# A recurrent scan with expert work in its gaps: the work one step later, and the first gate inputs taken from SBUF

## The chip, the cores and the metric

One NeuronCore of a Trainium2 chip runs the whole program. The metric is device time in microseconds (us), the median of several executions; lower is better.

## What is computed

The input x has 8 sequences of 512 tokens with 256 channels. First comes a mixture of experts with a residual: one shared gated MLP and, for each token, the best 2 of 8 small experts. Then a gated recurrent unit (GRU) runs over the 512 tokens of each sequence, again with a residual.

```python
shared = silu(xf @ w1) * (xf @ w3) @ w2
combine = top-2 gates of sigmoid(concat(xf, cond) @ router_W), normalised
h = gelu(einsum('nc,ech->enh', xf, W1e)); y = einsum('enh,ehc->enc', h, W2e)
x = x + (shared + einsum('ne,enc->nc', combine, y)) / 3
Xz, Xr, Xh = x @ Wxz.T + bxz, x @ Wxr.T + bxr, x @ Wxh.T + bxh
for t in range(512):                 # H is 8 x 256
    Z = sigmoid(Xz[t] + H @ Whz.T + bhz)
    R = sigmoid(Xr[t] + H @ Whr.T + bhr)
    H = Z * H + (1 - Z) * tanh(Xh[t] + (R * H) @ Whh.T + bhh)
    Y[t] = H @ Whq.T + bhq
x = x + Y
```

## The kernel before

**Tiles and steps.** The tokens are cut in 32 tiles; tile n holds 16 time steps (TS) of all 8 sequences, 128 rows. The scan has 512 steps, named by (n, s): step s, 0 to 15, of tile n. The expert work of a pair of tiles is laid in the gaps of the scan's steps, well ahead of the steps that need it.

**One step of the scan** (the functions `body` of each engine). TensorE (PE) makes the product for R into `r_bank` and that for Z into `zc_bank` (L1235), then runs a first filler (`fill_up`), then the third product from `rhT`, then a second filler (`fill_rest`). ScalarE (ACT) takes the tanh of R (L685) and of Z (L687), copies the gate inputs of the next step into `r_bank` (`seed_r`, L608), makes `a_row` (L696), takes the tanh of the third product (`t_h`, L705) and copies the other gate inputs (`seed_zc`, L616). VectorE (DVE) transposes `t_r` (L974), makes `rhT` (L977), transposes `a_row` into `factors` (L980), makes `terms` (L991), transposes `t_h` (L996) and updates the state with two scans into `hist` (L999). Each engine takes its instructions in this order, so a wait on one instruction holds all behind it.

**The order of the filler is written out by hand.** `place_of(n, s)` (L375) turns a step into a pair p and a slot r from 0 to 31, since a pair of tiles spans 32 steps:

```python
sp = s + TS * ((n + 1) % 2)
return (n + 1) // 2 + (sp >= FIRST_STEP), (sp - FIRST_STEP) % SPAN
```

FIRST_STEP is 6, so slot r lies in step s = (r + 6) mod 16. Tables by slot say what each slot holds: `UP_GAP2` gives 5 matmuls of the up projections (L1100), 6 in the slots of `SIX_UPS`, 3 in two; `DOWNS1` the down projections (L1073); `PROJ1` the gate input projection of a tile in slots 2 to 5 and 18 to 21; `BIAS2` its bias add on DVE after the state update of slots 3, 5, 19 and 21 (L855); `HIDDEN1` a DVE product (L812) between `factors` and `terms`, in slot 8 among others; `TANH1` = 25 a small tanh of the router on ACT ahead of `t_h` (L565). What is tied to s and not to r: `keep_states`, an ACT copy of the 16 states of the tile before, in step s = 0 ahead of `t_h` (L623); the wait for a tile's gate inputs.

**How gate inputs travel.** The projection leaves `xproj` in SBUF with a row for each token. SyncE's queue (SP) stores it in two halves (q = 0, 1) in DRAM (`store_inputs`, L466), waits until a half has landed, and loads it back with 4 DMAs in the layout that a step reads, `xs` (`gate_rows`, L472). It does that for the first 8 time steps of a tile and later for the other 8. `seed_r` of the next tile's first step lies in step s = 15 and waits for the first part:

```python
if last:
    act.wait_ge(xs_first, 16 * NG * (n + 2))
seed_r(*after)
```

So for every tile boundary the bias add in step s = 11 (slots 5 and 21) starts a chain of store, landing, load, landing, which must be done by ACT's `seed_r` in step s = 15.

**The head** runs tile 0's experts and much of tile 1's before step (0, 0): the down projections of slots 6 to 9, and the first 36 matmuls of the next pair's up projections (`FIRST_UPS`). Tile 0's gate inputs go the same way through DRAM, and SP loads the second part when the first has landed. In the tail, when no filler is left, `keep_busy` (L1239, L1243) gives PE two matmuls in a gap; a gap of slot 0 in tile 31 has none.

Of the kernel before, what the change touches and what calls it, by code (L numbers as in the profile page):

```python
# [17 lines left out]
def moe_then_gru(nc, x, cond, router_w, router_b, w1, w3, w2, we1, we2,  # L18
# [7 lines left out]
    B, T, C = x.shape  # L26
    P = 128
    TS = P // B
# [8 lines left out]
    NG = 4  # L37
    GW = C // NG
    Q = 32
# [6 lines left out]
    TOP_K = 2  # L46
    SHARE = 1.0 / (1 + TOP_K)
    HALF = TS // 2

    ctx = ExitStack()  # L50
    with ctx:
# [3 lines left out]
        def sem(name):  # L55
            return ctx.enter_context(nc.semaphore(name))
# [56 lines left out]
        xs = spent[:, 0:TS * RW].rearrange("p (t c) -> p t c", t=TS)  # L113
# [3 lines left out]
        xproj = spent[:, 0:NG * RW].rearrange("p (j c) -> p j c", j=NG)  # L117
# [28 lines left out]
        by_group = nc.dram_tensor("gate_inputs_by_group", [NG, P, RW], F32, kind="Internal").ap()  # L146
# [40 lines left out]
        xp_ready = sem("xp_ready")  # L187
        xp_stored = [sem(f"xp_stored{q}") for q in range(2)]
        xs_first = sem("xs_first")
        xs_second = sem("xs_second")  # L190

        bits_set = sem("bits_set")
        xs_zeroed = sem("xs_zeroed")
# [72 lines left out]
        def sig(p):  # L266
            return first_sig if p == 0 else later_sig
# [3 lines left out]

        UP_MM = 2 * KC * 3
        SPAN = 2 * TS
        FIRST_STEP = 6
        FIRST_R = SPAN - FIRST_STEP - TS
        NPAIR = NT // 2
        PIECES = 2
# [7 lines left out]
        UP_GAP2, begin = {}, 0  # L285
        for r in UP_ORDER:
            end = begin + (3 if r in X1_2 else 6 if r in SIX_UPS else 5)
            UP_GAP2[r] = range(begin, end)
            begin = end
# [33 lines left out]
        UP_ACT2 = {3: 0, 6: 1, 8: 2, 10: 3, 13: 4, 15: 5, 20: 6, 22: 7, 24: 8, 26: 9, 28: 10, 31: 11}  # L323
        SILU1 = {4: 0, 7: 1, 9: 2, 11: 3}
        HIDDEN1 = {5: 0, 8: 1, 10: 2, 12: 3}
        UP_ACT2_FIRST = {12: 3, 15: 4, 18: 5, 20: 6, 23: 7, 25: 8, 27: 9, 29: 10, 31: 11}
        SILU1_FIRST = {10: 2, 13: 3}
        HIDDEN1_FIRST = {11: 2, 14: 3}

# [10 lines left out]
        BASE1, TANH1 = 24, 25  # L340
        ROUTE_AHEAD1 = [r for r in range(26, SPAN) for _ in range(2)]
        ROUTE1 = [0, 1, 2, 6, 13, 14, 15, 16, 17, 18, 20, 21]
        FIRST_UPS = 36
        UP_FIRST, begin = {}, FIRST_UPS
        for r in [r for r in range(FIRST_R, SPAN - 1) if r not in LAST_DOWN2]:
            end = begin + (3 if r in X1_2 else 5 if r in LOGITS2 or r in (12, 13, 14, 25, 29) else 6)
            UP_FIRST[r] = range(begin, end)
            begin = end
# [20 lines left out]
        def turn(t, g):  # L369
            return NGR * t + g  # L370
# [4 lines left out]
        def place_of(n, s):  # L375

            sp = s + TS * ((n + 1) % 2)
            return (n + 1) // 2 + (sp >= FIRST_STEP), (sp - FIRST_STEP) % SPAN

# [19 lines left out]
        def _(sp):  # L399
# [62 lines left out]
            def store_inputs(t, q):  # L462

                groups = slice(q * NG // PIECES, (q + 1) * NG // PIECES)
                sp.wait_ge(xp_ready, PIECES * t + q + 1)
                sp.dma_start(by_group[groups, :, :].rearrange("j p c -> p j c"), xproj[:, groups, :]).then_inc(xp_stored[q], 16)  # L466

            def gate_rows(q, half, done):

                for j in range(q * NG // PIECES, (q + 1) * NG // PIECES):  # L470
                    src = by_group[j, :, :].rearrange("(b t) c -> b t c", b=B)[:, half * HALF:(half + 1) * HALF, :]
                    sp.dma_start(xs[Q * j:Q * j + B, half * HALF:(half + 1) * HALF, :], src).then_inc(done, 16)  # L472

            for q in range(PIECES):
                store_inputs(0, q)
            sp.wait_ge(xs_zeroed, 1)
            for q in range(PIECES):
                sp.wait_ge(xp_stored[q], 16)
                gate_rows(q, 0, xs_first)
            sp.wait_ge(xs_first, 16 * NG)  # L480
            for q in range(PIECES):
                gate_rows(q, 1, xs_second)
            load_late(EARLY + 1)
            sp.wait_ge(shared_ready, NSH)
            sp.wait_ge(we1_split, NE)
# [1 line left out]
            def store_out(t):  # L487

                sp.wait_ge(y_ready, t + 1)
                sp.dma_start(out[:, t * TS:(t + 1) * TS, :], y_out[:, :]).then_inc(out_stored, 16)  # L490
# [8 lines left out]
            def body(n, scan, proj, outs):  # L499
                if n % 2 == 0 and n > 0:  # L500
                    store_out(n - 2)
                if proj:
                    sp.wait_ge(xs_second, 16 * NG * (n + 1))
                    for q in range(PIECES):
                        store_inputs(n + 1, q)
                    sp.wait_ge(seeded_zc, TS * n + HALF)
                    for q in range(PIECES):
                        sp.wait_ge(xp_stored[q], 16 * (n + 2))
                        gate_rows(q, 0, xs_first)
                if n % 2 == 0 and 0 < n < NT:  # L510
                    store_out(n - 1)
                if proj:
                    sp.wait_ge(seeded_zc, TS * (n + 1))
                    for q in range(PIECES):
                        gate_rows(q, 1, xs_second)
                if n % 2 == 0 and n + EARLY + 2 < NT:
                    sp.wait_ge(late_xT_ready, n + 2)
                    load_late(n + EARLY + 2)
                    load_late(n + EARLY + 3)
# [29 lines left out]
        def _(act):  # L549
# [17 lines left out]
            def consume_up(p, place):  # L567

                u, ps = UNITS[place], up_ps[place % 2]
                act.wait_ge(up_done, len(UNITS) * p + place + 1)  # L570
                if u < 0:
                    act.activation(sig(p)[:, ~u, :], ps[:, 0:PAIR], ACT.Tanh, scale=0.5).then_inc(sig_done, 1)
                else:
                    if p > 0:
                        act.wait_ge(dn_done, turn(2 * p - 1, u + 1) + 1)
                    act.activation(hid_e[:, u, :, :].rearrange("p k t -> p (k t)"), ps[:, 0:2 * PAIR], ACT.Gelu)\
                       .then_inc(gelu_ready, 1)
# [90 lines left out]
            copy_x1T(0)  # L668
            consume_up(1, 0)
            consume_up(1, 1)  # L670
            act.wait_ge(xs_first, 16 * NG)
            seed_r(0, 0)
            seed_zc(0, 0)
            consume_up(1, 2)

            def body(n, scan, proj, outs):
                for s in range(TS):
                    p, r = place_of(n, s)
                    last = s + 1 == TS
                    after = (n, s + 1) if scan and not last else (n + 1, 0) if proj and last else None  # L680
                    if scan:
                        for i in range(NI):
                            if i == 0:
                                act.wait_ge(r_done, TS * n + s + 1)
                            act.activation(t_r[:, i, :], r_ps[:, i * Q:(i + 1) * Q], ACT.Tanh, scale=0.5).then_inc(tr_ready, 1)  # L685
                        act.wait_ge(z_done, TS * n + s + 1)
                        act.activation(t_z[:, :, :].rearrange("p i q -> p (i q)"), z_ps, ACT.Tanh, scale=0.5).then_inc(tz_ready, 1)  # L687
                    if after:
                        if s + 1 == HALF:
                            act.wait_ge(xs_second, 16 * NG * (n + 1))  # L690
                        if last:
                            act.wait_ge(xs_first, 16 * NG * (n + 2))
                        seed_r(*after)
                    if scan:
                        act.wait_ge(tz_ready, TS * n + s + 1)
                        act.activation(a_row[:, :, :], t_z[:, :, :], ACT.Copy, bias=0.5, scale=-0.5).then_inc(a_ready, 1)  # L696
                    if outs and n < NT and s == 0:
                        keep_states(n - 1)
                    if EARLY <= 2 * p + 2 < NT and r == TANH1:
                        score_tanh(p, slice(2 * p + 2, 2 * p + 4))  # L700
                    if scan:
                        for i in range(NI):
                            if i == 0:
                                act.wait_ge(c_done, TS * n + s + 1)
                            act.activation(t_h[:, i, :], c_ps[:, i * Q:(i + 1) * Q], ACT.Tanh, scale=-1.0).then_inc(th_ready, 1)  # L705
                    if (n, s) == (NT - 1, TS - 1):
                        keep_all_but_last()
                    if after:
                        seed_zc(*after)
                    if 0 <= p < NPAIR and r in first_or(p, UP_ACT2_FIRST, UP_ACT2):  # L710
                        consume_up(p, first_or(p, UP_ACT2_FIRST, UP_ACT2)[r])
                    if 0 < p + 1 < NPAIR and r == X_HIGH2:
                        split_x(p + 1)
                    if 0 < p <= NPAIR and r in X1_2:
                        copy_x1T(2 * p + X1_2[r])
# [304 lines left out]
        def _(pe):  # L1020
# [290 lines left out]
            for r in range(6, FIRST_R):  # L1311
                for _, g, tile, k, begin, end in DOWNS1[r]:
                    down(2 + tile, g, k, begin, end, full=True)
            for m in range(2 * UP_MM, FIRST_UPS):
                up(1, m)
# [53 lines left out]
```

## Time and profile before

| | us |
|---|---|
| median of 3 runs (1282.32 to 1283.2) | 1282.59 |
| the profiled execution, span from first to last instruction | 1282.1 |
| PE busy | 1255.5 (98%) |
| DVE busy | 996.5 (78%) |
| ACT busy | 805.1 (63%) |
| first step of the scan begins | 50.92 |
| last step of the scan begins | 1274.98 |

The profiled execution has no separate time of its own beside its span, and its span lies 0.5 us below the median of the runs. A busy PE is not a PE at its peak, since matmuls overlap. An idle time in brackets in a row stands ahead of the instruction, with what ended it.

### The profile page before, as it was taken

To read this page: it belongs to the slowest core of one execution; us is meant where nothing else is said; L and a number is where in the kernel's file an instruction comes from. 1 tells how busy PE (TensorE), PEld (TensorE's weight loads), DVE (VectorE), ACT (ScalarE), POOL (GpSimd) and SP (SyncE) were. 2 spreads that over 40 slices of the span, in tenths; PEclk is the share of its full clock that TensorE was granted. 3 is DMA by queue.
4 is the path that set the end of the run, shared out by engine and by line. 5 is a ranking of instruction groups with operands and counts; after the bars stand their busy time and mean duration, and the time that the engine had idled before them with its cause. 6 is when DMAs were issued, how large, how long until landed. Compare 5 with 4: busy or idle time off the path is not lost.

```text
span 1282.1 us, 84275 instructions
## 1 busy us (share of the span) xinstructions
PE 1255.5 (98%) x35592; PEld 879.3 (69%) x35592; DVE 996.5 (78%) x6111; ACT 805.1 (63%) x4402; POOL 7.4 (1%) x25
## 2 busy tenths in 40 slices
PE   9999999999999999999999999999999999999887
PEld 8876667766667766667767666766666766666554
DVE  6678787787787878778787887777877787877765
ACT  4366666666666666666666666666666666666554
POOL 1000000000000000000000000000000000000000
PEclk9999999999999999999999999999999999999999
DMA  9311011111101111011111101111011111000110
GB/s 272 59 33 44 23 40 27 42 40 34 39 20 42 35 37 45 24 37 27 43 40 34 38 21 43 33 38 45 27 33 27 44 39 33 23 21 26 33 32 11
DMA packets 76185, 51.34 MB, mean 40 GB/s; under 512 B 40608, under 2 KB 73760, under 8 KB 75808
## 3 DMA queue, kind: packets, MB, share of 16 engines
q1 hardware_dynamic: 75128, 45.29, 13.9%
q8 instruction: 281, 4.60, 1.5%
q14 instruction: 96, 0.79, 0.2%
q10 hardware_dynamic: 680, 0.66, 0.2%
HBM read 29.13 MB, written 16.78 MB: 36 GB/s over the span
## 4 chain that ended last, share of the span: by engine, by line
PE 93%; DVE 3%; ACT 2%; issue 1%; DMA 1%; SPq 0%
PE dn_ps L1073 27%; PE up_ps L1100 26%; PE zc_bank L1235 21%; PE r_bank L1235 15%; PE aux L1073 2%; DVE terms L996 2%; PE dn_ps L1107 1%; ACT t_h L705 1%; PE misc L1073 1%; DVE hist L999 1%; DMA x_all<-in_x 1%; ACT t_r L685 0%; DVE t_rT L974 0%; PE zc_bank L1048 0%; DVE rhT L977 0%
## 5 line engine op out<-in xcount | busy, mean ns | idle before, releaser
L974 DVE STREAM_TRANSPOSE t_rT<-t_r 128x32 f32<-128x32 f32 x1024 | 156.1, 191 | 176.6 <-ACT t_r L685 167.4
L685 ACT ACTIVATE t_r<-r_bank 128x32 f32<-128x32 f32 x1024 | 146.3, 195 | 213.9 <-PE r_bank L1235 201.5
L705 ACT ACTIVATE t_h<-zc_bank 128x32 f32<-128x32 f32 x1024 | 146.1, 195 | 208.2 <-PE zc_bank L1235 208.2
L1073 PE MATMUL dn_ps<-we_sb,x_all 128*32 128x256 f32 (+1 forms) x5144 | 274.8, 329 | 0.0
L1235 PEld LDWEIGHTS zc_bank<-whT,rhT 128*8 128x8 f32 x8192 | 118.2, 87 | 177.9 <-DVE rhT L977 176.9
L1235 PE MATMUL r_bank<-whT,hist 128*8 128x64 f32 x8192 | 210.1, 220 | 16.6 <-DVE hist L999 13.6
L1235 PE MATMUL zc_bank<-whT,rhT 128*8 128x64 f32 x8192 | 211.5, 220 | 2.7 <-DVE rhT L977 0.3
L1235 PE MATMUL zc_bank<-whT,hist 128*8 128x64 f32 x8192 | 208.9, 219 | 0.4 <-issue 0.4
L1235 PEld LDWEIGHTS r_bank<-whT,hist 128*8 128x8 f32 x8192 | 117.8, 88 | 111.5 <-DVE hist L999 92.7
L996 DVE STREAM_TRANSPOSE terms<-t_h 128x32 f32<-128x32 f32 x1024 | 156.5, 192 | 39.6 <-ACT t_h L705 20.7
L1073 PEld LDWEIGHTS dn_ps<-we_sb,x_all 128*32 128x32 f32 x5144 | 138.2, 110 | 31.0
L616 ACT ACTIVATE zc_bank<-gru_raw 128x128 f32<-128x128 f32 x512 | 144.3, 282 | 16.1
L1100 PE MATMUL up_ps<-x_high,we_high 128*128 128x256 f32 x512 | 153.4, 300 | 0.0
L1100 PE MATMUL up_ps<-x_high,we_low 128*128 128x256 f32 x512 | 152.4, 298 | 0.2 <-issue 0.2
L1100 PE MATMUL up_ps<-x_low,we_high 128*128 128x256 f32 x512 | 152.1, 297 | 0.0
L999 DVE TENSOR_TENSOR_SCAN hist<-factors,terms 128x16 f32<-128x16 f32 x1024 | 145.3, 183 | 0.0
L1235 PEld LDWEIGHTS zc_bank<-whT,hist 128*8 128x8 f32 x8192 | 142.5, 90 | 0.7 <-issue 0.6
L980 DVE STREAM_TRANSPOSE factors<-a_row 128x64 f32<-128x64 f32 x512 | 126.0, 246 | 20.1 <-ACT a_row L696 1.1
L977 DVE SCALAR_TENSOR_TENSOR rhT<-t_rT,hist 128x8 f32<-128x8 f32 x1024 | 133.2, 167 | 0.0
L696 ACT ACTIVATE a_row<-t_z 128x64 f32<-128x64 f32 x512 | 125.6, 245 | 0.0
L844 DVE SCALAR_TENSOR_TENSOR x_all<-dn_ps,gates_all,x_all 128x256 f32<-128x256 f32 x256 | 121.1, 473 | 5.8 <-PE dn_ps L1107 1.9
L608 ACT ACTIVATE r_bank<-gru_raw 128x64 f32<-128x64 f32 x512 | 114.0, 223 | 3.5 <-DMA gru_raw<-gate_inputs_by_group 3.5
(132 smaller groups left out, 1663.8 us busy)
## 6 DMA issues: line engine op xcount, KB each, us to landing
gate_inputs_by_group<-gru_raw SPq DMA_DIRECT2D x64, 192.0 KB, 2.0
gru_raw<-gate_inputs_by_group SPq DMA_DIRECT2D x256, 48.0 KB
xT_all<-in_x SPq DMA_DIRECT2D x448, 8.0 KB
x_all<-in_x SPq DMA_DIRECT2D x31, 128.0 KB
out<-gru_raw SPq DMA_DIRECT2D x31, 128.0 KB
x_all<-in_L_cond_W1e SPq DMA_DIRECT2D x4, 512.0 KB, 7.5
we_sb<-in_L_cond_W2e SPq DMA_DIRECT2D x4, 512.0 KB, 8.4
xT_all<-in_L_cond_w SPq DMA_DIRECT2D x2, 256.0 KB, 5.6
```

Of the source, the lines that this page charges most:

```text
L616: act.activation(zc_bank[:, 0:2 * GW], xs[:, s, GW:RW], ACT.Copy).then_inc(seeded_zc, 1)
L685: act.activation(t_r[:, i, :], r_ps[:, i * Q:(i + 1) * Q], ACT.Tanh, scale=0.5).then_inc(tr_ready, 1)
L696: act.activation(a_row[:, :, :], t_z[:, :, :], ACT.Copy, bias=0.5, scale=-0.5).then_inc(a_ready, 1)
L705: act.activation(t_h[:, i, :], c_ps[:, i * Q:(i + 1) * Q], ACT.Tanh, scale=-1.0).then_inc(th_ready, 1)
L974: dve.transpose(t_rT[:, i, :], t_r[:, i, :]).then_inc(trT_done, 1)
L977: dve.scalar_tensor_tensor(rhT[:, i, :], t_rT[:, i, 0:B], 1.0, old[:, i, :], ALU.add, ALU.mult)\
L980: dve.transpose(factors[:, :, :, 1].rearrange("p i q -> p (i q)"), a_row[:, :, :].rearrange("p i q -> p (i q)"))\
L996: dve.transpose(terms[:, i, :, 0], t_h[:, i, :]).then_inc(thT_done, 1)
L999: dve.tensor_tensor_scan(hist[:, s, i, :, :].rearrange("p b e -> p (b e)"), factors[:, i, 0:B, :].rearrange("p b e -> p (b e)"), terms[:, ...
L1073: done = pe.matmul(ps[Q * j:Q * (j + 1), col:col + cols], lhsT[:, Q * j:Q * (j + 1)], rhs, start=first, stop=last, tile_position=(0, Q * j ...
L1100: done = pe.matmul(up_ps[place % 2][:, half * PAIR:(half + 1) * PAIR], w, (x_low if low_x else x_high)[:, p % 2, :, k, :], start=(m % UP_M ...
L1235: done = pe.matmul(ps[Q * j:Q * j + B, :], lhsT[:, k, :], whT[:, gate, k, j * GW:(j + 1) * GW], start=False, stop=(k == NI - 1), tile_posi ...
```

## The change

All slots move one step later (`FIRST_STEP` 7), so slot r lies in step s = (r + 7) mod 16. Slot 9 of the first pair, with its down projections, 6 up matmuls and DVE's third add, moves from the head into step (0, 0), and so does ACT's use of the third up unit. The gate inputs of steps 0, 1 and 2 of tile 0 are copied by 12 small DMAs from `xproj` straight to `xs`, with a semaphore for each step; steps 3 to 7 and 8 to 15 go through DRAM as before, and SP no longer waits for the first part ahead of the second.

```diff
-        FIRST_STEP = 6
+        FIRST_STEP = 7
-        UP_ACT2_FIRST = {12: 3, 15: 4, ...}
+        UP_ACT2_FIRST = {9: 2, 12: 3, 15: 4, ...}
-        FIRST_UPS = 36
+        FIRST_UPS = 30
...
+            def step_rows(s, q):
+                for j in range(q * NG // PIECES, (q + 1) * NG // PIECES):
+                    sp.dma_start(xs[Q * j:Q * j + B, s, :], xproj[s::TS, j, :]).then_inc(xs_step[s], 16)
...
-            for q in range(PIECES):
-                store_inputs(0, q)
             sp.wait_ge(xs_zeroed, 1)
+            sp.wait_ge(xp_ready, 1)
+            step_rows(0, 0)
+            store_inputs(0, 0)
+            sp.wait_ge(xp_ready, 2)
+            step_rows(0, 1)
+            store_inputs(0, 1)
+            for s in range(1, AHEAD):
+                for q in range(PIECES):
+                    step_rows(s, q)
             for q in range(PIECES):
                 sp.wait_ge(xp_stored[q], 16)
-                gate_rows(q, 0, xs_first)
-            sp.wait_ge(xs_first, 16 * NG)
+                gate_rows(q, AHEAD, HALF, xs_first)
             for q in range(PIECES):
-                gate_rows(q, 1, xs_second)
+                gate_rows(q, HALF, TS, xs_second)
...
-            act.wait_ge(xs_first, 16 * NG)
+            act.wait_ge(xs_step[0], 16 * NG)
             seed_r(0, 0)
             seed_zc(0, 0)
-            consume_up(1, 2)
...
+                        if n == 0 and 0 < s + 1 < AHEAD:
+                            act.wait_ge(xs_step[s + 1], 16 * NG)
+                        if n == 0 and s + 1 == AHEAD:
+                            act.wait_ge(xs_first, 16 * NG)
```

The wait for the next tile's first part stays in step s = 15, and `keep_states` stays in step s = 0.

## Rows read from the trace of the kernel before

**Rows 1.** The page: shares of the chain that ended last.

```profile
PE 93%; DVE 3%; ACT 2%; issue 1%; DMA 1%; SPq 0%
```

**Rows 2.** Timeline of a step in the tail: start, length, instruction, idle before it.

```profile
1249.97 0.41 PE L1235 MATMUL r_bank<-whT,hist 128*8 128x64 f32 x16 [0.35 <-DVE hist L999]
...
1251.85 0.31 DVE L996 STREAM_TRANSPOSE terms<-t_h 128x32 f32<-128x32 f32 x2 [0.18 <-ACT t_h L705]
...
1252.35 0.41 PE L1235 MATMUL r_bank<-whT,hist 128*8 128x64 f32 x16 [0.35 <-DVE hist L999]
```

**Rows 3.** Timeline of PE and ACT, end of the head and first step.

```profile
46.80 2.79 PE L1107 MATMUL dn_ps<-we_sb,x_all 128*128 128x256 f32 x16
...
49.54 0.28 PE L1100 MATMUL up_ps<-x_low,w_high 128*128 128x256 f32 x1
...
50.40 0.23 ACT L608 ACTIVATE r_bank<-gru_raw 128x64 f32<-128x64 f32 x1 [3.46 <-DMA gru_raw<-gate_inputs_by_group]
...
50.72 0.28 PE L1100 MATMUL up_ps<-x_high,w_low 128*128 128x256 f32 x1
50.92 0.41 PE L1235 MATMUL r_bank<-whT,hist 128*8 128x64 f32 x16
...
53.34 0.41 PE L1235 MATMUL r_bank<-whT,hist 128*8 128x64 f32 x16
```

**Rows 4.** Timeline of SP in the head: issue and length of each DMA instruction.

```profile
43.73 0.39 SPq L466 DMA_DIRECT2D gate_inputs_by_group<-gru_raw  x1
...
45.02 0.38 SPq L466 DMA_DIRECT2D gate_inputs_by_group<-gru_raw  x1
...
47.02 0.60 SPq L472 DMA_DIRECT2D gru_raw<-gate_inputs_by_group  x2
...
50.39 0.26 SPq L472 DMA_DIRECT2D gru_raw<-gate_inputs_by_group  x1
```

**Rows 5.** SP and ACT at one boundary (tile 26); SP's waits, landings at all 31.

```profile
1076.39 0.38 SPq L466 DMA_DIRECT2D gate_inputs_by_group<-gru_raw  x1
...
1078.42 0.60 SPq L472 DMA_DIRECT2D gru_raw<-gate_inputs_by_group  x2
...
1083.93 0.23 ACT L608 ACTIVATE r_bank<-gru_raw 128x64 f32<-128x64 f32 x1
...
SPq L472 <- DMA gate_inputs_by_group<-gru_raw: 35.1, 31, 2.6
...
DMA to landing us min/median/max: 2.0/2.0/3.7
```

**Rows 6.** Timeline of DVE: step s = 15 of tile 26, and a step of slot 8.

```profile
1084.65 0.18 DVE L991 SCALAR_TENSOR_TENSOR terms<-factors,hist 128x16 f32<-128x16 f32 x1
1084.97 0.31 DVE L996 STREAM_TRANSPOSE terms<-t_h 128x32 f32<-128x32 f32 x2
...
1044.10 0.16 DVE L991 SCALAR_TENSOR_TENSOR terms<-factors,hist 128x16 f32<-128x16 f32 x1
1044.27 0.31 DVE L996 STREAM_TRANSPOSE terms<-t_h 128x32 f32<-128x32 f32 x2
```

**Rows 7.** Timeline of ACT: router tanh in slot 25, copy of states in s = 0.

```profile
241.42 0.20 ACT L565 ACTIVATE score<-logits 128x16 f32<-128x16 f32 x1
...
243.75 0.63 ACT L623 ACTIVATE gru_raw<-hist 128x256 f32<-128x256 f32 x1
...
244.29 0.28 ACT L705 ACTIVATE t_h<-zc_bank 128x32 f32<-128x32 f32 x2
```

**Rows 8.** Timeline of PE and a window of all engines in tile 31 (PEclk ahead of DMA).

```profile
1254.72 0.41 PE L1235 MATMUL r_bank<-whT,hist 128*8 128x64 f32 x16 [0.79 <-DVE hist L999]
...
1257.10 0.61 PE L1235 MATMUL r_bank<-whT,hist 128*8 128x64 f32 x16 [0.36 <-DVE hist L999]
...
1260.73 0.40 PE L1235 MATMUL r_bank<-whT,hist 128*8 128x64 f32 x16
...
1257.20:1260.60 3.40, 3.40 (x66) 2.28 (x64) 1.46 (x10) 1.36 (x8) 0.00 (x0) 0.50 0.02 5
```

More of the change, by code:

```diff
@@ L48, in moe_then_gru @@
     HALF = TS // 2
+    AHEAD = 3
     ctx = ExitStack()
@@ L190, in moe_then_gru @@
         xs_second = sem("xs_second")
+        xs_step = [sem(f"xs_step{s}") for s in range(AHEAD)]
         bits_set = sem("bits_set")
@@ L325, in moe_then_gru @@
         HIDDEN1 = {5: 0, 8: 1, 10: 2, 12: 3}
-        UP_ACT2_FIRST = {12: 3, 15: 4, 18: 5, 20: 6, 23: 7, 25: 8, 27: 9, 29: 10, 31: 11}
+        UP_ACT2_FIRST = {9: 2, 12: 3, 15: 4, 18: 5, 20: 6, 23: 7, 25: 8, 27: 9, 29: 10, 31: 11}
         SILU1_FIRST = {10: 2, 13: 3}
@@ L466, in store_inputs, with gate_rows @@
                 sp.dma_start(by_group[groups, :, :].rearrange("j p c -> p j c"), xproj[:, groups, :]).then_inc(xp_stored[q], 16)
-            def gate_rows(q, half, done):
+            def gate_rows(q, begin, end, done):
                 for j in range(q * NG // PIECES, (q + 1) * NG // PIECES):
-                    src = by_group[j, :, :].rearrange("(b t) c -> b t c", b=B)[:, half * HALF:(half + 1) * HALF, :]
-                    sp.dma_start(xs[Q * j:Q * j + B, half * HALF:(half + 1) * HALF, :], src).then_inc(done, 16)
-            for q in range(PIECES):
-                store_inputs(0, q)
-            sp.wait_ge(xs_zeroed, 1)
+                    src = by_group[j, :, :].rearrange("(b t) c -> b t c", b=B)[:, begin:end, :]
+                    sp.dma_start(xs[Q * j:Q * j + B, begin:end, :], src).then_inc(done, 16)
+            def step_rows(s, q):
+                for j in range(q * NG // PIECES, (q + 1) * NG // PIECES):
+                    sp.dma_start(xs[Q * j:Q * j + B, s, :], xproj[s::TS, j, :]).then_inc(xs_step[s], 16)
+            sp.wait_ge(xs_zeroed, 1)
+            sp.wait_ge(xp_ready, 1)
[7 more added lines that the diff above has]
+                    step_rows(s, q)
             for q in range(PIECES):
                 sp.wait_ge(xp_stored[q], 16)
-                gate_rows(q, 0, xs_first)
-            sp.wait_ge(xs_first, 16 * NG)
+                gate_rows(q, AHEAD, HALF, xs_first)
             for q in range(PIECES):
-                gate_rows(q, 1, xs_second)
+                gate_rows(q, HALF, TS, xs_second)
             load_late(EARLY + 1)
@@ L508, in body @@
                         sp.wait_ge(xp_stored[q], 16 * (n + 2))
-                        gate_rows(q, 0, xs_first)
+                        gate_rows(q, 0, HALF, xs_first)
                 if n % 2 == 0 and 0 < n < NT:
@@ L514, in body @@
                     for q in range(PIECES):
-                        gate_rows(q, 1, xs_second)
+                        gate_rows(q, HALF, TS, xs_second)
                 if n % 2 == 0 and n + EARLY + 2 < NT:
```

## The prediction

> **What bounds the kernel now.** I read the page first. PE is 98% busy by the table and holds 93% of the chain that ended last [rows 1], which suggests that PE's work sets the time. The timeline of a step in the tail corrects that: there nearly all filler is gone, PE idles 0.35 us ahead of the state's next product, and the step still takes 1252.35 - 1249.97 = 2.38 us [rows 2]. A step with a full load of 6 up matmuls takes 53.34 - 50.92 = 2.42 [rows 3]. So a step is bound by its own round trip PE, ACT, DVE, PE, ACT, DVE; the filler hides in it. The mean over the scan is (1274.98 - 50.92) / 511 = 2.395. What remains outside is the head, 50.9 us. Next I read SP's queue and ACT at a tile boundary, because the change leaves one wait where it is (ACT's, in step s = 15) and moves what it waits for. The reader is to see how little time lies between the two.
>
> **The head: 1.36 us less.** PE is back to back up to the scan. Six up matmuls leave it: ten pitches lie between 49.54 and 50.72, 0.118 each, so 0.71. The downs of slots 6 to 9 run from 46.80 to 49.42 (the second up matmul less one pitch); slot 9 holds 3 of their 12 half-width pieces, a quarter of 2.62, so 0.65. The scan would begin at 50.92 - 1.36 = 49.56 [rows 3]. DVE's add and ACT's third up unit, which move too, lie behind the state update and `seed_zc` in step 0, where other steps hide the same work.
>
> **Is the first gate input there?** Before, ACT waited 3.46 us for the DMA and had it at 50.40, 0.5 ahead of PE's need [rows 3]: without the direct copies the gain would be lost. Now the store issues show xproj's halves ready at 43.73 and 45.02, and an issue takes about 0.34 with its gap. Step 0's last copy issues at 45.4. The trace has no SBUF to SBUF copy; the nearest rows are the store, 2.0 to landing [rows 5], and the load, last issued at 47.32 and landed at 50.39, 3.07 [rows 4]. So it lands at 47.4 to 48.4, ahead of 49.56 either way: nothing. On SP the queue then holds the second store and 8 more copies: step 1's last issues at 47.2 and lands at 49.2 to 50.2, wanted at 49.56 + 0.8 = 50.4; if each issue took 0.47 it would be 0.6 late. I take nothing, and keep 0 to 0.6. Step 2's is wanted one step later and has 1.2 more. The loads of steps 3 to 7 issue by 49.9, land by 53.0 and are wanted at 55.2. The second part and the x loads behind it issue by 51.7, as before, since 12 issues fill what was SP's wait up to 50.39 [rows 4].
>
> **One more full step in place of a light one:** slot 9 costs step 0 its 2.42 for a light 2.38: +0.04.
>
> **The hand-over at each tile boundary: 12.2 us more.** This is the step on which all rests. The bias add that releases the second store moves from step 11 to 12, and ACT's wait stays in step 15. At tile 26 the store issues at 1076.39, SP sees it land and issues the two last loads from 1078.42, the second at 1078.72; with 3.07 to landing that is 1081.79. ACT's `seed_r` runs at 1083.93 [rows 4, 5]. The margin is 2.14, and the change takes 2.39 of it: 0.25 late in a clean hand-over. Not all are clean: SP's wait for the store is 35.1 / 31 = 1.13 in the mean, at tile 26 it is about 0.9, and the longest is 2.6; a landing took up to 3.7 against 2.0 [rows 5]. So 0.23 more in the mean, 0.48 late in all. What does a late `seed_r` hold? Behind it on ACT stand `a_row` and `t_h`, and DVE waits for `a_row` to make `factors` and `terms`, ahead of the transposes of `t_h`. In the 16 boundaries after even tiles `terms` is done 0.14 ahead of the transposes [rows 6]; with the overlap of issue I give it 0.17 of cover, so 0.31 each, 5.0 in all. After the 15 odd tiles step 15 now holds slot 8, whose DVE product lies between `factors` and `terms`, and the transposes follow `terms` with no gap (1044.10 + 0.16, then 1044.27) [rows 6]: no cover, 0.48 each, 7.2. Sum 12.2. The bounds: if a load landed as fast as a store (2.0) the clean margin would be 3.2 and only the worst of the delays would be left, some 2 us in all; if every load took 3.7, 0.6 more at each of 31 boundaries gives 32. I take the 3.07, the only landing of these same loads that an engine was seen to wait for.
>
> The Trainium skill, in "DMA: Bandwidth & Descriptors" (Anatomy of one DMA), gives a DMA a fixed cost of about 2.0 us, most of it the receipt of the last byte, plus its bytes at 436 GB/s. Its fit is for DMAs issued from GpSimd. By it these loads would land after an estimated 2.1 us, the hand-over would still be in time and the sum would fall to about 1284. The store's row agrees with it, the load's 3.07 doesn't, and the measurement decides here.
>
> **Two ACT extras in one step: 1.4 us more.** After odd tiles, step s = 0 now holds slot 25: the router's tanh joins the copy of the states, both ahead of `t_h`. The copy alone already leaves ACT no idle time before `t_h`, which starts 0.54 after it [rows 7], where a light step has slack. Of the tanh's 0.20 about 0.10 overlaps with its neighbour, as with the copy (0.63 against 0.54). 14 pairs are routed in the scan: 14 x 0.10 = 1.4, bounds 0 and 2.8. Elsewhere slots meet the same neighbours as before.
>
> **The clock.** After a gap without `keep_busy` PE idled 0.79 and then ran at a granted clock of 0.50 of full, the 1.2 GHz level, for 3.4 us; that step took 1260.73 - 1257.10, or 3.64 for 2.38: 1.26 more [rows 8]. The same gap comes one step later; I leave it in. A long stall at a boundary idles PE for as long and could do likewise in a full step. Only hand-overs that are late by over 1 us would. The longest wait for a store, 2.6 against 0.9 [rows 5], says that there are such; I guess three, 1.3 to 1.7 each, which is 0 to 5 us, and take none.
>
> **The sum.** -1.36 + 0.04 + 12.2 + 1.4 = +12.3 on the profiled 1282.1 is 1294.4; the runs' median lies 0.5 higher, so **1295 us**, 1.0% slower.
>
> **The rivals.**
> - *The hand-over is still in time.* For it: an unhindered boundary is only 0.25 short by a price taken once, in the head. It decides at a landing of about 2.8 us; below that clean boundaries don't stall. Then -1.36 + 0.04 + 1.4 + 2 for the worst ones: 1284.7, or 1281.3 if the tanh is hidden and no landing is late. This is the case that isn't slower. Against it: only 2.39 less than 2.14 in a clean one, and the mean wait shows that many aren't clean.
> - *The stalls also drop PE's clock.* For it: 0.79 us of idle did so in the tail. Against it: the full steps around a boundary are much busier than those of the tail. Price three times 1.3 to 1.7 over the sum: 1299 to 1300.
> - *The start doesn't come earlier,* because step 0's or 1's copies land late. It decides at a landing of over 4 us for step 0. Then 1.36 is lost: 1296.5, within the range.
>
> **How the numbers follow.** The change within 0.2% (2.6 us) can't be told from none. The forecast with its own range of 1288 to 1300 has 0.78; the stalls with a lower clock 0.10; the start not earlier 0.03; the hand-over in time 0.09, of which 0.01 falls below 1280.0, 0.06 within 2.6 us and 0.02 just above. So faster 0.01, same 0.07, slower 0.92 with the rest. The range takes in the clock's case and most of the price's bounds, and leaves out the hand-over in time: 1287 to 1303.
>
> **What would show it.** In the changed kernel's profile the scan's first product starts near 49.6. Waits of ACT `r_bank` L608 (its new line) on the DMA of the gate inputs appear about 31 times, once in 16 steps, with a sum of 12 to 18 us; steps s = 15 last 2.4 to 4.5 and vary, more so after odd tiles; steps s = 0 after odd tiles, 14 of them, last 2.48. All others stay at 2.38 to 2.43. If ACT shows no such waits, the load's price was wrong; if PE's clock falls at boundaries, the second rival holds. A stall that DVE or PE absorbs would leave the waits but not the long steps, and the prediction would fail at its cover.

## Result and the profile after

The changed kernel takes **1299.24 us** (median of 4 runs, 1298.13 to 1301.93) against 1282.89 us for the kernel before (4 runs, 1282.32 to 1286.08): ratio 1.0125, interval 1.0111 to 1.014. It is 1.3% slower. The prediction was 1295 us, range 1287 to 1303. The profiled execution spans 1297.2 us against 1282.1, 15.1 more.

The page's chain of the kernel after, shares by engine and the first shares by line:

```profile
PE 77%; DMA 9%; DVE 7%; ACT 5%; issue 1%; SPq 1%; DVEq 0%
PE dn_ps L1089 22%; PE up_ps L1116 21%; PE zc_bank L1251 17%; PE r_bank L1251 13%; DMA gru_raw<-gate_inputs_by_group 5%; DMA gate_inputs_by_group<-gru_raw 3%; DVE terms L1012 2%; PE aux L1089 2%; DVE hist L1015 1%; ACT t_h L721 1%; ACT t_r L697 1%; PE dn_ps L1123 1%; ACT a_row L712 1%; PE misc L1089 1%; DVE factors L996 1%
```

Before, DMA had 1% of the chain and PE 93% [rows 1]. Now 9% goes by way of the gate inputs' DMAs: their store and load have become the end of a chain. The waits say who stands there. The view of the kernel after gives sum, count and longest, all in us:

```profile
DVE factors L996 <- ACT a_row L712: 21.2, 33, 2.0
...
ACT r_bank L621 <- DMA gru_raw<-gate_inputs_by_group: 14.6, 16, 1.8
...
PEld up_ps L1116 <- DVE hid L828: 11.7, 14, 2.0
...
ACT r_bank L621 <- DMA gru_raw<-gru_raw: 1.6, 3, 1.0
...
SPq L474 <- DMA gate_inputs_by_group<-gru_raw: 35.8, 31, 2.4
```

ACT's `seed_r` (its line is now L621) waits for the loads (of the 16 waits that the view lists, one, 0.6 us, is in the head; it leaves out the short ones), `factors` on DVE waits for ACT, and PE's filler waits for DVE's product `hid` behind that. In the scan of the kernel before, ACT waited for a tile's first part nowhere. Now `seed_r` starts 0.02 us after the last of these loads has landed at each of the 31 boundaries, by the semaphore's updates in the trace. SP's own wait for the store has hardly moved: 35.8 / 31 = 1.15 us in the mean against 1.13 [rows 5].

Windows over steps s = 15 of the kernel after, 16 with even n and then 15 with odd n. Columns as in [rows 8]: bounds, length, busy time of PE, PEld, DVE, ACT and POOL, PEclk, DMA share, GB/s.

```profile
243.38:247.24 3.86, 2.48 (x79) 1.83 (x79) 1.81 (x14) 1.71 (x9) 0.00 (x0) 1.00 0.33 92
...
sum 42.28, PE 38.41 PEld 28.84 DVE 29.76 ACT 25.59 POOL 0.00; mean PE 2.40 PEld 1.80 DVE 1.86 ACT 1.60 POOL 0.00
...
201.92:206.15 4.23, 2.57 (x70) 1.79 (x70) 2.10 (x14) 1.60 (x9) 0.00 (x0) 1.00 0.52 86
...
sum 47.35, PE 38.19 PEld 26.50 DVE 30.91 ACT 24.63 POOL 0.00; mean PE 2.55 PEld 1.77 DVE 2.06 ACT 1.64 POOL 0.00
```

The same view of the kernel before, over its steps s = 14 (even n, odd n). They held the slots that s = 15 holds now, so they are the right measure:

```profile
sum 38.42, PE 37.95 PEld 28.75 DVE 30.32 ACT 23.42 POOL 0.00; mean PE 2.37 PEld 1.80 DVE 1.89 ACT 1.46 POOL 0.00
...
sum 36.03, PE 35.66 PEld 26.40 DVE 31.00 ACT 21.70 POOL 0.00; mean PE 2.38 PEld 1.76 DVE 2.07 ACT 1.45 POOL 0.00
```

Even boundaries cost 42.28 - 38.42 = 3.9 us more, odd ones 47.35 - 36.03 = 11.3: **15.2 us together**, the whole of the difference. The other parts cancel each other. One of the worst, tile 3, in the timeline of DVE, ACT and PE:

```profile
202.62 0.22 ACT L699 ACTIVATE t_z<-zc_bank 128x64 f32<-128x64 f32 x1
...
204.56 0.23 ACT L621 ACTIVATE r_bank<-gru_raw 128x64 f32<-128x64 f32 x1 [1.71 <-DMA gru_raw<-gate_inputs_by_group]
204.72 0.24 ACT L712 ACTIVATE a_row<-t_z 128x64 f32<-128x64 f32 x1
204.99 0.25 DVE L996 STREAM_TRANSPOSE factors<-a_row 128x64 f32<-128x64 f32 x1 [1.85 <-ACT a_row L712]
205.16 0.38 DVE L828 TENSOR_TENSOR hid<-gru_raw,up_ps 128x256 f32<-128x256 f32 x1
205.47 0.16 DVE L1007 SCALAR_TENSOR_TENSOR terms<-factors,hist 128x16 f32<-128x16 f32 x1
205.54 0.29 DVE L1012 STREAM_TRANSPOSE terms<-t_h 128x32 f32<-128x32 f32 x2
205.60 0.39 PE L1116 MATMUL up_ps<-x_high,w_high 128*128 128x256 f32 x1 [1.66 <-DVE hid L828]
```

This is the chain that the prediction described: `seed_r`, `a_row`, `factors`, slot 8's product, `terms`, the transposes of `t_h`, with no gap between.

### The profile page after: what moved, and what is told of

It is laid out like the page before. It is cut to its first block, busy times and chain, and to the rows that moved or that the text cites. A ratio compares the mean times of both kernels' runs of the same rounds, so it can differ in the third digit from the quotient of the medians.

```text
span 1297.2 us, 84306 instructions
## 1 busy us (share of the span) xinstructions
PE 1257.4 (97%) x35600; PEld 878.5 (68%) x35600; DVE 995.9 (77%) x6111; ACT 805.6 (62%) x4402; POOL 7.4 (1%) x25
## 4 chain that ended last, share of the span: by engine, by line
PE 77%; DMA 9%; DVE 7%; ACT 5%; issue 1%; SPq 1%; DVEq 0%
PE dn_ps L1089 22%; PE up_ps L1116 21%; PE zc_bank L1251 17%; PE r_bank L1251 13%; DMA gru_raw<-gate_inputs_by_group 5%; DMA gate_inputs_by_group<-gru_raw 3%; DVE terms L1012 2%; PE aux L1089 2%; DVE hist L1015 1%; ACT t_h L721 1%; ACT t_r L697 1%; PE dn_ps L1123 1%; ACT a_row L712 1%; PE misc L1089 1%; DVE factors L996 1%
## 5 line engine op out<-in xcount | busy, mean ns | idle before, releaser
L621 ACT ACTIVATE r_bank<-gru_raw 128x64 f32<-128x64 f32 x512 | 114.3, 223 | 17.4 <-DMA gru_raw<-gate_inputs_by_group 14.6
```

## Experiments

The kernel before ran 11 times beside the first four experiments, with a median of 1282.17 us (1281.33 to 1285.45), and 23 times beside the last four, 1283.14 (1280.51 to 1286.11). Ratios are against those.

**E1, the wait one step earlier, nothing else.** The kernel before, its slots and head untouched; only ACT's wait for the next tile's first part goes from s = 15 to s = 14. This takes the same 2.39 us out of the same hand-over.

```diff
-                        if last:
+                        if s + 2 == TS and proj:
                             act.wait_ge(xs_first, 16 * NG * (n + 2))
```

> The kernel before with one edit: ACT's wait for the next tile's gate inputs stands in step s = 14 and not 15. No slot moves, the head is the old one. If the lost margin at the tile boundary is the cause (theory), this alone costs as much as the whole change or a little more: 15 to 19 us over the kernel before (about 1299 to 1301), with some 31 waits of ACT's r_bank copy on the DMA, long steps s = 14, longer after odd tiles. If the cause is how the shifted slots meet what is tied to s, the new first steps or the head (rival), it costs nothing: within 2 us of before.

Measured: 1298.12 us (1296.01 to 1299.94), ratio 1.0122, 1.0107 to 1.0136: 16.0 us more. Its waits (the longest, 3.8, is that of the head), and its steps s = 14 with even and with odd n:

```profile
ACT r_bank L608 <- DMA gru_raw<-gate_inputs_by_group: 20.6, 21, 3.8
```

```profile
sum 43.92, PE 38.48 PEld 28.87 DVE 29.18 ACT 26.03 POOL 0.00; mean PE 2.40 PEld 1.80 DVE 1.82 ACT 1.63 POOL 0.00
...
sum 47.64, PE 38.01 PEld 26.44 DVE 30.92 ACT 24.71 POOL 0.00; mean PE 2.53 PEld 1.76 DVE 2.06 ACT 1.65 POOL 0.00
```

They grew by 5.5 and 11.6 us over the same steps of the kernel before, 17.1 together, and the shape is that of the change: the odd boundaries pay twice what the even ones pay. A margin of one step, taken away, costs all that the change costs, without any of its other parts. The rival of this test, slots that meet badly, had it at nothing.

**E2, step 0's row copied directly at every boundary.** The other side of the test: the changed kernel, with its slots as they are, but the row that s = 15 waits for no longer goes through DRAM. ACT waits for the rest one step later.

```diff
+                        sp.wait_ge(xp_ready, PIECES * (n + 1) + q + 1)
+                        step_rows(0, q)
                         store_inputs(n + 1, q)
...
-                        gate_rows(q, 0, HALF, xs_first)
+                        gate_rows(q, 1, HALF, xs_first)
...
+                        if n > 0 and s == 0:
+                            act.wait_ge(xs_first, 16 * NG * (n + 1))
                         if last:
-                            act.wait_ge(xs_first, 16 * NG * (n + 2))
+                            act.wait_ge(xs_step[0], 16 * NG * (n + 2))
```

> The changed kernel, but at every tile boundary step 0's gate inputs are also copied from SBUF to SBUF (4 more DMAs for each tile), and ACT waits for the loads from DRAM one step later, in step s = 0. The theory: the copies land about 1.7 us after their issue, two steps ahead of need, so the waits and the long steps s = 15 vanish and 16 to 17 us come back: 1282 to 1285. What is left over the kernel before is -1.3 (head), +0.9 (first three steps), +1.3 (router tanh beside the copy of states): +0.9. The rival, slots that meet badly: 1295 or more.

Measured: 1286.71 us (1285.24 to 1290.31), ratio 1.0036, 1.0023 to 1.0048. 12.5 us came back, 2 to 5 less than wanted. Its windows: steps s = 15 with even and odd n, then steps s = 0 with even n.

```profile
sum 38.58, PE 38.12 PEld 28.96 DVE 30.55 ACT 24.28 POOL 0.00; mean PE 2.38 PEld 1.81 DVE 1.91 ACT 1.52 POOL 0.00
...
sum 36.58, PE 36.22 PEld 26.39 DVE 30.97 ACT 22.89 POOL 0.00; mean PE 2.41 PEld 1.76 DVE 2.06 ACT 1.53 POOL 0.00
...
sum 41.29, PE 37.68 PEld 26.67 DVE 30.91 ACT 30.05 POOL 0.00; mean PE 2.35 PEld 1.67 DVE 1.93 ACT 1.88 POOL 0.00
```

The stalls in s = 15 are gone (75.16 against the 74.45 of the kernel before). But s = 0 now takes 41.29 where the kernel before had 38.07: ACT waits there for the remaining loads at four boundaries, 0.3 to 0.7 us each. In SP's queue the second store now stands behind the new copies; E5 tries whether that is the reason.

**E3, E2 with the router's tanh one slot later** (`TANH1` 25 to 26), so that it and the copy of the states lie in different steps.

> e2_direct_at_every_boundary with the router's tanh in slot 26 and not 25, so that it no longer lies in step s = 0 beside the copy of the states. The theory: steps s = 0 after odd tiles fall from 2.47 to 2.42 us (slot 26 has moved to s = 1 and is bound by PE at 2.42 anyway), so 14 x 0.09 = 1.3 us less than e2. The rival, that this pair costs nothing on the path: within 0.3 us of e2.

Measured: 1287.49 us (1284.4 to 1290.58), ratio 1.0037, 1.0022 to 1.0051. The 1.3 us less that were expected don't show in the median, which can't tell them with this spread. The steps can: those of slot 25 in s = 0 went from a median of 2.509 to 2.404 us. ACT in such a step, of the changed kernel and of E3:

```profile
90.08 0.63 ACT L636 ACTIVATE gru_raw<-hist 128x256 f32<-128x256 f32 x1
90.62 0.20 ACT L578 ACTIVATE score<-logits 128x16 f32<-128x16 f32 x1
90.72 0.26 ACT L721 ACTIVATE t_h<-zc_bank 128x32 f32<-128x32 f32 x2
```

```profile
90.09 0.63 ACT L638 ACTIVATE gru_raw<-hist 128x256 f32<-128x256 f32 x1
90.62 0.26 ACT L725 ACTIVATE t_h<-zc_bank 128x32 f32<-128x32 f32 x2
```

The tanh puts `t_h` back by 0.10 us, as predicted.

**E4, slots later but tile 0 through DRAM.** The changed kernel without its direct copies; only `FIRST_STEP`, the head's share of the work and the tables differ from the kernel before.

```diff
+            for q in range(PIECES):
+                store_inputs(0, q)
             sp.wait_ge(xs_zeroed, 1)
-            sp.wait_ge(xp_ready, 1)
-            step_rows(0, 0)
...
-                gate_rows(q, AHEAD, HALF, xs_first)
+                gate_rows(q, 0, HALF, xs_first)
+            sp.wait_ge(xs_first, 16 * NG)
```

> The changed kernel without the direct copies: all slots one step later, but tile 0's gate inputs go through DRAM as before. The theory: ACT gets them at about 50.4 us, so the scan starts near 50.7 and not 49.64, but steps 0 to 2 lose their waits for the copies (0.9 us): within 1 us of the changed kernel, about 1299. The rival, that the direct copies are worth the 1.3 us of the head: 1 to 2 us slower than the changed kernel.

Measured: 1300.39 us (1298.03 to 1301.38), ratio 1.0138, 1.0123 to 1.0153. That is 1.2 us above the changed kernel, between what the theory and its rival had, and the spread of the two doesn't decide. Its first products do:

```profile
50.84 0.41 PE L1241 MATMUL r_bank<-whT,hist 128*8 128x64 f32 x16 [1.04 <-ACT r_bank L615]
53.26 0.41 PE L1241 MATMUL r_bank<-whT,hist 128*8 128x64 f32 x16
```

Without the copies PE waits 1.04 us for the gate inputs and starts at 50.84, as the third rival said of such a case. With them it starts at 49.64, but the next three steps take 8.22 us for 7.25 here. So the direct copies move the start by 1.20 and give back 0.97, and 0.2 is left of them: the theory's case.

**E5, the second store ahead of its copies.** E3 with SP's order at a boundary mended for what E2 showed.

```diff
-                        step_rows(0, q)
+                        if q == 0:
+                            step_rows(0, q)
                         store_inputs(n + 1, q)
+                        if q == 1:
+                            step_rows(0, q)
```

> e3_direct_and_tanh_later with the order on SP changed at the boundaries: the second half's store is issued ahead of its two direct copies, not behind them (1.2 us earlier). In e3 what was left over the kernel before is 4 to 5 us; steps s = 0, where ACT now waits for the loads from DRAM, hold 3 of them. The theory of the hand-over margin: these loads then land 1.2 us earlier and steps s = 0 fall back, 2 to 3 us less than e3, 1284 to 1285. If the four more copies for each tile cost by themselves (rival): no change, 1287.

Measured: 1283.97 us (1282.57 to 1286.27, 11 runs), ratio 1.0007, 0.9999 to 1.0016. Steps s = 0 with even n fall to 38.72 us, from 41.29 in E2 and 40.87 in E3. Of the waits for loads one is left, and it is in the head; at the boundaries there is none:

```profile
ACT r_bank L626 <- DMA gru_raw<-gate_inputs_by_group: 0.5, 1, 0.5
```

**E6, GpSimd's queue issues the copies of steps 1 and 2 of tile 0.** E5 with these 8 copies off SP.

```diff
-            for s in range(1, AHEAD):
-                for q in range(PIECES):
-                    step_rows(s, q)
...
+            pool.wait_ge(xs_zeroed, 1)
+            for q in range(PIECES):
+                pool.wait_ge(xp_ready, q + 1)
+                for s in range(1, AHEAD):
+                    for j in range(q * NG // PIECES, (q + 1) * NG // PIECES):
+                        pool.dma_start(xs[Q * j:Q * j + B, s, :], xproj[s::TS, j, :]).then_inc(xs_step[s], 16)
```

> e5_store_before_copies with the 8 copies for steps 1 and 2 of tile 0 issued by GpSimd's queue and not by SP's. The theory: the waits of steps 0 to 2 come from SP's issue time of 0.6 us for each copy; with two queues they vanish (steps 0 to 2 at 2.38 to 2.42 each and not 2.60, 2.61 and 2.7 to 3.0), 0.7 to 0.9 us less than e5. The rival: it is the landing and not the issue, then nothing changes or it grows.

Measured: 1284.1 us (1281.57 to 1286.05, 12 runs), ratio 1.0006, 0.9998 to 1.0015. The time is that of E5. The trace did what was expected, in PE's and POOL's timelines:

```profile
43.80 4.41 POOL L566 DMA_DIRECT2D gru_raw<-gru_raw  x8 [7.90 <-DVE gru_raw L881]
```

```profile
49.05 0.41 PE L1261 MATMUL r_bank<-whT,hist 128*8 128x64 f32 x16
51.46 0.41 PE L1261 MATMUL r_bank<-whT,hist 128*8 128x64 f32 x16
```

The first steps are back at 2.41 us and the scan starts 1.9 us before that of the kernel before. Still the kernel isn't faster than before. In its trace the two steps around a boundary (s = 15 and 0) take some 0.03 us more each than the steps that held the same slots before (s = 14 and 15), 1.9 us in all. One part may be that `seed_r` stands 0.85 us into a step where it follows a wait that is already over, and 0.82 where it follows none. That was not tested, and what holds the kernel at its old time stays open: the profiled execution, 1281.57 us, is the fastest of the 12.

**E7, two steps later, steps 0 and 1 direct.** Is there more to gain the same way? `FIRST_STEP` is 8, `FIRST_UPS` 24, and at each boundary the rows of steps 0 and 1 by direct copies, with a semaphore of its own for step 1.

```diff
-        FIRST_STEP = 7
+        FIRST_STEP = 8
-        FIRST_UPS = 30
+        FIRST_UPS = 24
...
+                        step_rows(0, q)
                         if q == 0:
-                            step_rows(0, q)
+                            step_rows(1, q, xs_row1)
```

> e6_pool_issues_copies with all slots one step later still (first step 8, 24 up matmuls in the head) and the direct copies extended to steps 0 and 1 of each tile. The theory: the head loses another 1.36 us of PE work and the hand-over is still in time by some 0.4 us where nothing disturbs it; landings that are late by more cost: 0 to 1.4 us less than e6 if few are late, up to 5 more if many are. The scan starts near 48.3 to 48.6.

Measured: 1290.11 us (1287.35 to 1291.31), ratio 1.0049, 1.0037 to 1.0061: 6 us more than E6. That is a little worse than the worse of the two cases expected. The scan starts at 48.82, but now the direct copies themselves are late: of the 9 waits below two are in the head and 7, with 7.6 us, at boundaries.

```profile
ACT r_bank L631 <- DMA gru_raw<-gru_raw: 9.3, 9, 1.7
```

**E8, the wait two steps earlier.** E1 with `s + 3 == TS`: every boundary is late by at least one step, so the price per microsecond of lateness and the clock's behaviour after long stalls show apart from jitter.

> The kernel before with ACT's wait for the next tile's gate inputs in step s = 13, twice the dose of e1. The theory: with the margin of some 1.9 us used up by the first step, each further step costs nearly its whole 2.39 us at each of 31 boundaries: 74 us over e1, and the even ones lose their cover of 0.25 no second time: 1370 to 1378. If something else than the margin made e1 slow (rival), the second step costs no more than the first: about 1314.

Measured: 1398.52 us (1393.79 and 1403.25, 2 runs), ratio 1.0897, 1.0864 to 1.0929; the profiled span is 1391.9 us, 109.8 over the kernel before. The forecast of 1370 to 1378 was 20 us short or more. Its wait, and windows over three stalled steps, each followed by the next step:

```profile
ACT r_bank L608 <- DMA gru_raw<-gate_inputs_by_group: 95.9, 32, 4.3
```

```profile
82.24:86.86 4.62, 2.55 (x79) 1.84 (x78) 1.92 (x12) 1.71 (x9) 0.00 (x0) 1.00 0.12 33
86.86:90.72 3.86, 3.86 (x70) 2.95 (x71) 2.32 (x14) 1.40 (x9) 0.00 (x0) 0.56 0.00 0
...
254.58:259.40 4.82, 2.55 (x79) 1.84 (x78) 1.90 (x12) 1.64 (x9) 0.00 (x0) 1.00 0.24 68
259.40:261.82 2.42, 2.42 (x71) 1.84 (x71) 1.96 (x14) 1.48 (x9) 0.00 (x0) 1.00 0.00 0
```

Steps s = 13 took 163.5 us for 73.9 of before, 89.6 more, where 31 x 2.39 = 74.1 on E1's 17.1 makes 91.2: a stall costs its lateness, one for one. The rest is the clock. After 14 of the 31 stalls the next step lasted over 2.9 us, as at 86.86, where the granted clock was 0.56; steps s = 14 and 15 together took 21.5 us more than before. After others, as at 259.40, it stayed at full. The stalled steps were of the same lengths in both cases, 4.6 to 6.7 us with a slow step behind them and 4.6 to 6.2 without, so length alone doesn't decide it.

## Why the prediction was right, and where it was off

The span's 15.1 us by steps, of the two profiled executions:

| part | predicted | measured |
|---|---|---|
| start of the scan, 50.92 to 49.64 | -1.36 | -1.28 |
| first three steps, 7.31 to 8.22 | +0.04 | +0.91 |
| s = 15, even n, 38.06 to 42.28 | +5.0 | +4.2 |
| s = 15, odd n, 35.65 to 47.34 | +7.2 | +11.7 |
| s = 0, odd n, 38.65 to 39.43 | +1.4 | +0.8 |
| s = 0, even n, 35.62 to 37.06 | 0 | +1.4 |
| tile 31, 34.51 to 33.25 | 0 | -1.3 |
| all other steps, 1034.25 to 1032.89 | 0 | -1.4 |

The rows of s = 15 compare with the steps s = 15 of before, 15.9 us in all; against the steps that held the same slots it is the 15.2 of above.

**The mechanism was right and was shown from both sides.** E1 makes the loss with the wait alone; E2 takes the boundary stalls away with the slots left where the change put them. The rival of a hand-over still in time is refuted: at each of the 31 boundaries `seed_r` comes when the loads have landed and later in its step than in steps that wait for nothing.

**The hand-over term was too small: 12.2 us against 15.2.** The working had 0.25 us late for a clean boundary and 0.23 in the mean for disturbed ones. By `seed_r`'s place in its step (0.83 us in, where nothing holds it), 20 boundaries were late by 0.03 to 0.31, 0.18 in the mean, so the clean part was about right. The other 11 hold 14.2 of the 17.9 us of lateness. The mean is 0.58 instead of 0.48. The one price for the loads, 3.07, held in the mean: the last load was at ACT after 3.04. The term that was mis-sized is the 0.23 that I took from SP's wait. From the issue of the second store to that of the last load, tile 26 of the kernel before took 1078.72 - 1076.39 = 2.33 us [rows 5], but its 31 boundaries 2.65 in the mean, which is 0.32 more. In the changed kernel the mean is 2.62.

Of the 14.2 us, 9.8 lie at six boundaries whose second store landed after 3.0 to 3.5 us and not 2.0, and 4.4 at five whose last load took 3.4 to 4.0. Here is one of each, with a clean one. Tile 3's second store was issued at 197.68. What moved between 197.7 and 199.7:

```profile
q8 instruction: 1, 0.02, 4.6%
...
gate_inputs_by_group<-gru_raw SPq DMA_DIRECT2D x1, 192.0 KB, 3.4
```

SP issued the last load of tile 15 in the middle of this row and ACT got it here:

```profile
669.36 1.81 SPq L474 DMA_DIRECT2D gru_raw<-gate_inputs_by_group  x2
```

```profile
673.63 0.23 ACT L621 ACTIVATE r_bank<-gru_raw 128x64 f32<-128x64 f32 x1 [1.16 <-DMA gru_raw<-gate_inputs_by_group]
```

With the usual 0.31 between issues that load went out at 669.66 and took 3.97 us to ACT. At tile 26, a clean one, the second store is issued at 1094.64. Between 1094.6 and 1096.6 no packet of q8 moves, and the store lands after 2.0 us (first row). The same pair of loads goes out in the second row and is at ACT in the third, 1099.89 - 1096.96 = 2.93 later:

```profile
gate_inputs_by_group<-gru_raw SPq DMA_DIRECT2D x1, 192.0 KB, 2.0
```

```profile
1096.65 0.61 SPq L474 DMA_DIRECT2D gru_raw<-gate_inputs_by_group  x2
```

```profile
1099.89 0.23 ACT L621 ACTIVATE r_bank<-gru_raw 128x64 f32<-128x64 f32 x1
```

A packet of q8, which the page lists as the queue of instructions, goes with the late stores in every trace. Of the 620 stores at boundaries in the ten traces, 145 had such a packet start 0.15 to 1.5 us after their issue. These landed after 2.7 to 4.1 us, 3.2 in the median; of the other 475, with a median of 2.0, seven took over 2.7. The packets are of 16 KB and take 1.1 us in the median. No run moved them. That they delay the stores is therefore read from the times and was not tested. The five late loads of the changed kernel had one on its way too, but so had 18 of the 26 others. The late stores also keep their places: tiles 3, 8, 13, 18 and 23 in the changed kernel and in E4, tiles 1, 6, 11, 16, 21 and 25 in the kernel before and in E1, which have the same slots.

The Trainium skill, in "DMA: Bandwidth & Descriptors" (Anatomy of one DMA), would have each of these loads land after an estimated 2.1 us by its fixed cost and size; in these rows neither does. For the store's 192 KB its fit gives an estimated 2.45 us where the clean one took 2.0, so the store's row agrees with the fixed cost of about 2.0 and not, as the prediction had it, with the whole.

**The two parities differ more than the working had it.** Cover was near what I gave: a boundary 0.59 late (tile 6) grew by 0.34, so 0.25 was hidden where I had 0.17, and odd ones hide nothing (11.3 late, 11.3 longer than the steps with the same slots). The even ones together were 6.6 late and 3.9 longer, 0.17 hidden each. But I took 0.48 late for both, and it was 0.41 after even tiles and 0.76 after odd ones. E1 has the same split, 9.0 and 11.5 us of lateness. Of the six late stores three followed odd tiles, of the five late loads four. What sets the split stays open.

**"I take nothing" for steps 1 and 2 was wrong by 0.9.** SP's queue in the head, and ACT's `seed_r` there:

```profile
43.88 1.27 SPq L479 DMA_DIRECT2D gru_raw<-gru_raw  x2
...
45.67 1.19 SPq L479 DMA_DIRECT2D gru_raw<-gru_raw  x2
...
47.40 4.84 SPq L479 DMA_DIRECT2D gru_raw<-gru_raw  x8
```

```profile
48.01 0.23 ACT L621 ACTIVATE r_bank<-gru_raw 128x64 f32<-128x64 f32 x1 [0.99 <-DMA gru_raw<-gru_raw]
50.95 0.23 ACT L621 ACTIVATE r_bank<-gru_raw 128x64 f32<-128x64 f32 x1 [0.38 <-DMA gru_raw<-gru_raw]
53.37 0.23 ACT L621 ACTIVATE r_bank<-gru_raw 128x64 f32<-128x64 f32 x1 [0.21 <-DMA gru_raw<-gru_raw]
56.39 0.23 ACT L621 ACTIVATE r_bank<-gru_raw 128x64 f32<-128x64 f32 x1 [0.62 <-DMA gru_raw<-gate_inputs_by_group]
```

A direct copy takes SP 4.84 / 8 = 0.6 us to issue, not the 0.34 of a load or the 0.47 that I allowed as worst. The landing was inside my range (issued at about 46.3, at ACT by 48.01: 1.7). So step 0's input was early, as predicted, and each later one was behind a queue of issues; the loads of steps 3 to 7 were behind it too.

**The clock.** It fell once in the scan, after tile 3's stall: PE idled 1.66 us in that step and the next one took 206.15 to 209.95, 3.80 for 2.38. A window of the kernel after:

```profile
206.50:209.90 3.40, 3.40 (x57) 2.57 (x45) 2.06 (x12) 1.91 (x9) 0.00 (x0) 0.51 0.04 13
```

That is the 1.2 GHz level for 3.4 us, +1.4. The stalls of tiles 4, 13, 18 and 23, 1.5 to 1.9 us late, had none. In E1 five stalls of 1.7 to 2.2 us had none either. I had guessed three such falls at 1.3 to 1.7 and priced them at nothing. The fall in the tail [rows 8] is absent after the change, which gives 1.3 back, so the two cancel within the spans. That isn't the change's doing: E1 has the tail of the kernel before, with the same gap, and no fall there, and none of the other traces has one. So "I leave it in" was wrong by 1.3. The second rival had three falls: the change has one, E8 has many. The working looked for falls behind hand-overs over 1 us late; one of eight such had one.

**The tanh** puts `t_h` back by 0.10 us, and moved away it makes its 14 steps 0.105 shorter (E2 to E3), 1.4 in all, as predicted. But from the kernel before to the changed one the steps s = 0 after odd tiles grew by 0.05 each in the median, from 2.416 to 2.465, and by 0.8 in all. The working set 2.48 against a usual 2.38, and these steps took 2.42 before already.

**In the chances** the 0.06 for a change within 2.6 us became 0.07 in the last line, and 0.93 for slower became 0.92. Nothing else rests on it.

**From span to median** I added 0.5. A run's time is 1.8 to 1.9 us above its own span, and the profiled execution of before was a long one: the 11 runs of the first batch spanned 1279.5 to 1283.6 us, around 1280.3. So the medians differ by 16.35 us and the spans by 15.15, and the 1.2 between them is of no part of the change; the fall in the tail of the profiled one (1.26) would account for it, but the other runs have no trace to show that.

## What to carry to other kernels

Where a change moves a producer and leaves its consumer's wait, work out the slack of that hand-over first, and for the disturbed cases as well as the clean one: here 2.14 us of margin against a move of 2.39 left none of 31 boundaries with time to spare, and 11 of them held four fifths of the lateness. Take the spread from all instances of the hand-over, issue to issue, and not from one wait in it. Work taken out of a head is worth its length once; a margin taken from a repeated hand-over is paid each time (-1.3 against +15.2). When a transfer is split in small DMAs to start sooner, count their issues on the queue and what is queued behind them.

## What was not expected of the hardware

- A copy of 8 rows from SBUF to SBUF took SP 0.6 us to issue, twice a load from DRAM that brings 8 steps at once (0.31). GpSimd's queue issued 8 in 4.41 us, 0.55 each.
- A direct copy was at ACT 1.7 us after its issue, a load from DRAM 2.9 in a clean case and 4.0 in a disturbed one.
- A store of 192 KB landed 2.0 us after its issue, but after 2.7 to 4.1 in each of the 145 cases, of 620, in which a 16 KB packet of the instruction queue started 0.15 to 1.5 us after that issue. Nothing was run to move those packets.
- Stalls of 1.5 to 1.9 us in an otherwise busy stretch dropped PE's granted clock to half after one of five (0.51 for 3.4 us), and in E1 after none of five of 1.7 to 2.2; stalls in steps of 4.6 to 6.7 us (E8) after 14 of 31.
